# A four-layer graph kernel on Trainium2: gcn_first transposes its own rows, VectorE joins them, ScalarE scales the residual's part

## The reference, cut to what matters

```
def gcn_layer(x, edge_index, W, b, num_nodes):      # its own self loops are added once more
    deg  = segment_sum(1, dst);  dinv = rsqrt(deg);  norm = dinv[src] * dinv[dst]
    h    = x @ W
    return segment_sum(h[src] * norm, dst) + b
h   = relu(gcn_layer(x, edge_index, W1, b1))        # 128 -> 256
out = gcn_layer(h, edge_index, W2, b2)              # 256 -> 128
x   = layernorm(x + out)
```

## Time and profile before

| what | value |
|---|---|
| median of the runs | 5544.67 us |
| profiled execution | 5548.76 us |
| its span | 5547.0 us |
| mean granted TensorE clock | 0.932 |
| TensorE matmul busy | 4744.4 us (86%) |
| VectorE busy | 3861.5 us (70%) |
| GpSimd busy | 3017.4 us (54%) |
| ScalarE busy | 2782.1 us (50%) |

### The profile page before, as it was taken

One profiled execution on the slowest core, in us unless ns is written; L12 is line 12 of the kernel. 1 busy time (PEld: TensorE's weight loads), 2 busy tenths in 40 slices (PEclk: granted clock), 3 DMA queues, 4 the chain that ended last, 5 costly groups with the idle time before them and its releaser, 6 DMA issues. The chain is left out here.

```text
span 5547.0 us, 105377 instructions
## 1 busy us (share of the span) xinstructions
PE 4744.4 (86%) x27509; PEld 3749.1 (68%) x27509; DVE 3861.5 (70%) x11930; ACT 2782.1 (50%) x6703; POOL 3017.4 (54%) x2962
## 2 busy tenths in 40 slices
PE   4499996666799989999999997898799999447887
PEld 4488885555688867777777775777566666227887
DVE  8577775776688855555555554788688888885766
ACT  3644444656333322222222222788677777793545
POOL 0077765777677743333334333777466664007776
PEclk9999998777899989999999998999899999558999
DMA  4889994554577754444444443788877775784554
GB/s 149 274 246 275 273 270 142 151 147 147 177 237 238 236 170 151 153 154 150 150 147 153 152 153 92 223 250 249 245 221 222 222 225 181 261 294 132 153 148 141
DMA packets 551178, 1075.23 MB, mean 194 GB/s; under 512 B 110995, under 2 KB 118202, under 8 KB 547962
## 3 DMA queue, kind: packets, MB, share of 16 engines
q1 hardware_dynamic: 451194, 854.46, 46.5%
q0 software_dynamic: 99840, 219.14, 16.0%
HBM read 712.24 MB, written 360.98 MB: 193 GB/s over the span
## 5 line engine op out<-in xcount | busy, mean ns | idle before, releaser
L841 POOL DMA_INDIRECT s_rows<-t_h,s_index x416 | 525.4, 1263 | 831.5 <-DVE s_index L834 730.5
L841 POOL DMA_INDIRECT cb_rows<-t_x,cb_index x416 | 395.7, 951 | 451.4 <-DVE cb_index L834 327.7
L841 POOL DMA_INDIRECT g_rows<-t_x,g_index x416 | 425.9, 1024 | 384.9 <-issue 366.5
L841 POOL DMA_INDIRECT at_rows<-t_m,at_index x416 | 435.6, 1047 | 299.1 <-DVE at_index L834 189.8
L841 POOL DMA_INDIRECT s_rows<-t_v,s_index x416 | 405.1, 974 | 211.4 <-issue 120.4
L841 POOL DMA_INDIRECT s_rows<-t_x,s_index x416 | 420.5, 1011 | 154.8 <-issue 117.9
L841 POOL DMA_INDIRECT g_rows<-t_h,g_index x416 | 403.1, 969 | 171.1 <-issue 124.7
L905 PE MATMUL bank<-s_onehot,s_hi 128*128 128x80 f32 (+9 forms) x1758 | 436.7, 288 | 48.8 <-DVE s_lo L876 26.6
L1724 DVE TENSOR_TENSOR s_rout<-bank,s_x 128x512 f32<-128x512 f32 x98 | 67.9, 693 | 587.1 <-PE bank L1668 587.1
L905 PE MATMUL bank<-g_onehot,g_rows 128*128 128x80 f32 (+9 forms) x1172 | 299.6, 420 | 199.5 <-DMA g_rows<-t_h,g_index 193.5
L905 PE MATMUL bank<-s_onehot,s_lo 128*128 128x80 f32 (+9 forms) x1758 | 431.0, 285 | 0.0
(11 more groups left out here) (334 smaller groups left out, 13011.1 us busy)
## 6 DMA issues: line engine op xcount, KB each, us to landing
s_scale<-inv_d SPq DMA_DIRECT2D x196, 256.0 KB
t_h<-s_hout SPq DMA_DIRECT2D x98, 512.0 KB
s_own<-t_h SPq DMA_DIRECT2D x98, 512.0 KB
t_m<-s_mout SPq DMA_DIRECT2D x98, 264.0 KB
at_own<-t_m SPq DMA_DIRECT2D x98, 264.0 KB
t_x<-so_x SPq DMA_DIRECT2D x98, 256.0 KB, 4.7
g_own<-t_x SPq DMA_DIRECT2D x98, 256.0 KB
g_scale<-dinv_d SPq DMA_DIRECT2D x98, 256.0 KB
```

Of the source, the lines that this page charges most:

```text
L841: pool.indirect_dma_start(out=self.rows[:, self.ring(q) + k, :], out_offset=None, in_=self.table[0:NPAD, :], in_offset=bass.IndirectOffset ...
```

## The change

`gcn_first` no longer adds its own rows by products. TensorE transposes them into `bank[5]` (`flip`), ScalarE copies them to one of four SBUF tiles `own_t` (`turn`), and `scale_sums` becomes two instructions on VectorE: own_t times own1 plus the bank, then times the scale row. Because bank 5 is now taken, `down` uses bank 4 for every group. ScalarE's `scale` writes both `hout` and `rout` (with the new factor `dinv3_n` = own1 * dinv * dinv), eight instructions, and waits for the stores of both tiles; `rest` on VectorE becomes two plain additions. The lists of TensorE and ScalarE are reordered; VectorE's and SyncE's keep their lags.

```
-                dve.tensor_scalar(dinv2_n[:, :], dinv_n[:, :], own1[:, 0:1], None, ALU.mult)
+                dve.scalar_tensor_tensor(out=dinv3_n[:, :], in0=dinv_n[:, :], scalar=own1[:, 0:1],
+                                         in1=dinv_n[:, :], op0=ALU.mult, op1=ALU.mult)
...
+            own_t = ph.pair("own_t", [P, GRP], n=4)
...
-                    (0, lambda q: load(sp, q, own_rows[q.u][:, :], own_group(t_x0, q.t), loaded[q.u], e.summed)),
+                    (0, lambda q: load(sp, q, own_rows[q.u][:, :], own_group(t_x0, q.t), loaded[q.u], owned)),
...
+                def flip(q):
+                    pe.wait_ge(loaded[q.u], q.n * 16 + 16)
+                    if not (isinstance(q.t, int) and q.t < 1):
+                        pe.wait_ge(turned, q.t)
+                    for b in range(BLK):
+                        last = pe.transpose(bank[5][:, b * P:(b + 1) * P], own_rows[q.u][:, b * D:(b + 1) * D],
+                                            ident[:, :])
+                    last.then_inc(owned, 1)
+
                 def sums(q):
                     e.fetched(pe, q)
-                    pe.wait_ge(loaded[q.u], q.n * 16 + 16)
                     if not is_first(q.t):
                         pe.wait_ge(agged, q.t - 1)
-                    e.sum_by_feature(pe, q, [bank[q.u]], close=False)
-                    for b in range(BLK):
-                        last = pe.matmul(nodes(bank[q.u])[:, b, :], own_rows[q.u][:, b * D:(b + 1) * D],
-                                         id_own1[:, :], start=False, stop=(b == BLK - 1),
-                                         skip_group_check=True)
-                    last.then_inc(e.summed, 1)
+                    e.sum_by_feature(pe, q, [bank[q.u]]).then_inc(e.summed, 1)
...
                 def down(q):
                     pe.wait_ge(relued, q.t + 1)
-                    if not is_first(q.t):
-                        pe.wait_ge(scaled, q.t - 1)
+                    if not (isinstance(q.t, int) and q.t < 1):
+                        pe.wait_ge(scaled, q.t)
                     for b in range(BLK):
                         for h in range(2):
-                            last = pe.matmul(bank[4 + q.u][:, b * D:(b + 1) * D],
+                            last = pe.matmul(bank[4][:, b * D:(b + 1) * D],
...
-                over_groups(pe, [(1, sums), (5, down), (3, up)])
+                over_groups(pe, [(1, sums), (3, up), (5, down), (0, flip)])
...
+                def turn(q):
+                    act.wait_ge(owned, q.t + 1)
+                    if not is_first(q.t, 4):
+                        act.wait_ge(agged, q.t - 3)
+                    act.activation(own_t[q.r][:, :], bank[5][:, :], ACT.Copy).then_inc(turned, 1)
...
                     act.wait_ge(lowered, q.t + 1)
                     if not is_first(q.t):
                         act.wait_ge(st_h[q.u], q.n * 16)
-                        act.wait_ge(rested, q.t - 1)
-                    for b in range(BLK):
-                        last = act.activation(hout[q.u][:, b * D:(b + 1) * D],
-                                              bank[4 + q.u][:, b * D:(b + 1) * D], ACT.Copy,
-                                              scale=col(dinv_n, q.t * BLK + b))
+                        act.wait_ge(st_r[q.u], q.n * 16)
+                    for to, by in ((hout, dinv_n), (rout, dinv3_n)):
+                        for b in range(BLK):
+                            last = act.activation(to[q.u][:, b * D:(b + 1) * D], bank[4][:, b * D:(b + 1) * D],
+                                                  ACT.Copy, scale=col(by, q.t * BLK + b))
                     last.then_inc(scaled, 1)

-                over_groups(act, [(4, relu), (6, scale), (0, lambda q: e.take_hi(act, q))])
+                over_groups(act, [(6, scale), (1, turn), (4, relu), (0, lambda q: e.take_hi(act, q))])
...
                 def scale_sums(q):
+                    dve.wait_ge(turned, q.t + 1)
                     dve.wait_ge(e.summed, q.t + 1)
+                    if not is_first(q.t):
+                        dve.wait_ge(hidden, q.t - 1)
+                    dve.scalar_tensor_tensor(out=planes(agg[q.u]), in0=planes(own_t[q.r]), scalar=own1[:, 0:1],
+                                             in1=nodes(bank[q.u]), op0=ALU.mult, op1=ALU.add).then_inc(link, 1)
+                    dve.wait_ge(link, q.t + 1)
                     dve.wait_ge(loaded_s[q.u], q.n * 16 + 16)
-                    if not is_first(q.t):
-                        dve.wait_ge(hidden, q.t - 1)
-                    dve.tensor_tensor(planes(agg[q.u]), nodes(bank[q.u]), planes(scale_row[q.u]), ALU.mult)\
+                    dve.tensor_tensor(agg[q.u][:, :], agg[q.u][:, :], scale_row[q.u][:, :], ALU.mult)\
                        .then_inc(agged, 1)

                 def rest(q):
                     dve.wait_ge(scaled, q.t + 1)
                     dve.wait_ge(loaded_x[q.u], q.n * 16 + 16)
-                    if not is_first(q.t):
-                        dve.wait_ge(st_r[q.u], q.n * 16)
-                    for b in range(BLK):
-                        f = slice(b * D, (b + 1) * D)
-                        last = dve.scalar_tensor_tensor(out=rout[q.u][:, f], in0=hout[q.u][:, f],
-                                                        scalar=col(dinv2_n, q.t * BLK + b),
-                                                        in1=xin[q.u][:, f], op0=ALU.mult, op1=ALU.add)
-                    last.then_inc(link, 1)
-                    dve.wait_ge(link, q.t + 1)
+                    dve.tensor_tensor(rout[q.u][:, :], rout[q.u][:, :], xin[q.u][:, :], ALU.add).then_inc(link2, 1)
+                    dve.wait_ge(link2, q.t + 1)
                     dve.tensor_tensor(rout[q.u][:, :], rout[q.u][:, :],
                                       b2_r[:, :, :].rearrange("p b f -> p (b f)"), ALU.add)\
                        .then_inc(rested, 1)
```

More of the change, by code:

```diff
@@ L222, in build_program @@
     dinv_n = sb("dinv_n", [P, T * BLK])
-    dinv2_n = sb("dinv2_n", [P, T * BLK])
+    dinv3_n = sb("dinv3_n", [P, T * BLK])
     inv_n = sb("inv_n", [P, T * BLK])
@@ L1304, in gcn_first @@
             agged, relued, scaled, rested = ph.sem("agged"), ph.sem("relued"), ph.sem("scaled"), ph.sem("rested")
-            hidden, lowered, link = ph.sem("hidden"), ph.sem("lowered"), ph.sem("link")
+            hidden, lowered, link, link2 = ph.sem("hidden"), ph.sem("lowered"), ph.sem("link"), ph.sem("link2")
+            owned, turned = ph.sem("owned"), ph.sem("turned")
             st_h, st_r = ph.sems("stored_h"), ph.sems("stored_r")
@@ L1387, in scale_sums @@
                 def scale_sums(q):
+                    dve.wait_ge(turned, q.t + 1)
                     dve.wait_ge(e.summed, q.t + 1)
-                    dve.wait_ge(loaded_s[q.u], q.n * 16 + 16)
                     if not is_first(q.t):
                         dve.wait_ge(hidden, q.t - 1)
-                    dve.tensor_tensor(planes(agg[q.u]), nodes(bank[q.u]), planes(scale_row[q.u]), ALU.mult)\
+                    dve.scalar_tensor_tensor(out=planes(agg[q.u]), in0=planes(own_t[q.r]), scalar=own1[:, 0:1],
+                                             in1=nodes(bank[q.u]), op0=ALU.mult, op1=ALU.add).then_inc(link, 1)
+                    dve.wait_ge(link, q.t + 1)
+                    dve.wait_ge(loaded_s[q.u], q.n * 16 + 16)
+                    dve.tensor_tensor(agg[q.u][:, :], agg[q.u][:, :], scale_row[q.u][:, :], ALU.mult)\
                        .then_inc(agged, 1)
```

## The result

The changed kernel took 6125.73 us (median of five runs, 6124.42 to 6133.81), the kernel before 5546.14 beside it (five runs). The ratio is 1.1053, with a 95% interval of 1.104 to 1.1065: slower by 10.5%, 580 us. The forecast was 6050, with a range of 5920 to 6180. On a second chip of the same speed the changed kernel took 6124.43 us, ratio 1.1049 (1.103 to 1.1067). The profiled execution took 6133.81 us, its span is 6132.0.

A forecast was written before the change was run, and what follows sets the result against it. TensorE and GpSimd were both taken as full before; the loop's 91 x 11.2 = 1019 us, plus 31 and 10, end the stage at 1368 instead of 862, +505 us: median 5544.7 becomes 6050, range 5920 to 6180.

The forecast's parts named there:

- period: In gcn_first, one turn of the loop from scale to scale: 11.2 us, against 5.5 to 5.8 before.
- landing: In gcn_first's loop, from issue of the rout store until it has landed and releases the next scale: 3.4 us.
- five last periods: In gcn_first, scale(93) to scale(97), without take_hi, lo or turn: 5 x 6.1 = 31 us.
- last scale to the next stage: At gcn_first's end: 8.9 us before the change, 10 with four more instructions.
- The bound and the mechanism: In gcn_first, scale(q+1) waits for the store of rout(q-1), a loop within one period, engines mostly waiting: +505 us.
- The bounds of the landing: For gcn_first's rout store: 2.0 us below, 4.7 us above, giving 5915 to 6175 us for the program.
- rival a: In gcn_first, the loop holds and TensorE joins it at a lower clock: some 100 us more, 6150 to 6200; chance 0.10.
- The 38 us that TensorE was to save: In gcn_first, four transposes replace eight products' weight loads: 0.39 us less for each of 98 groups, gone in the loop.
- at least nothing, at most 26 us: VectorE's cost in gcn_first: net +0.27 us a group, 26 us over 98 groups if it were the bound.
- Rival (b): In gcn_first, the store has landed when scale comes and GpSimd is the bound: +10 us, 5555; chance 0.05.
- 30 us for longer gathers: In gcn_first, four VectorE instructions with two SBUF inputs instead of two lengthen gathers: 416 x 0.073 = +30 us.
- Rival (c): In gcn_first, faster: TensorE's 38 us come back whole, 5507 us; chance 0.03.

The follow-up runs named there:

- e1b: Changed kernel with four buffers of rout in place of two, on chip A: 5540.17 us, ratio 0.9997 to the kernel before.
- e5: Changed kernel with SyncE issuing the store of rout ahead of the load of x and store of hout, chip A: 5823.5 us, ratio 1.0506.
- e4b: Changed kernel with own rows added by products again, no transposes or join, residual still on ScalarE, chip C: 6917.78 us, ratio 1.0432.
- e4: Changed kernel with own rows added by products again, no transposes or join, residual still on ScalarE, chip B: 6829.31 us, ratio 1.044.
- e1: Changed kernel with four buffers of rout in place of two, on chip B: 6578.98 us, ratio 1.0079 to the kernel before.

## Why the prediction was right, step by step

| step | forecast | one period | mean over 91 |
|---|---|---|---|
| ScalarE: scale, turn, relu, high part | 4.42 | 4.43 (803.29 to 807.72) | 4.36 |
| VectorE: low part, two additions | 2.08 | 2.19 (807.72 to 809.91) | 2.08 |
| SyncE: to the issue of the rout store | 1.29 | 1.29 (809.91 to 811.20) | 1.25 |
| landing, to the next scale | 3.4 | 4.64 (811.20 to 815.84) | 4.47 |
| period | 11.2 | 12.55 | 12.16 (305.79 to 1412.37) |
| five last periods | 31 | | 26.5 (to 1438.8) |
| last scale to the next stage | 10 | | 8.0 |

**The bound and the mechanism** held: GpSimd and TensorE no longer set the time, but a loop does that no engine's busy time shows, and e1b, which opens just that loop, gives back all of the slowdown. **The mis-sized term is the landing.** The step "I take 3.4, near the row with the same three transfers in the same order" used the stage's end, where the trace has a load of x 0.9 us behind the store and the next store 2.4 us behind, and where no gather has run since 817.8 us. In the steady period the loads of the own rows and of the scale row follow 0.7 and 1.3 us behind, gathers run, and it is 4.5 (4.3 from the issue until the store has landed). That accounts for the miss: 1.07 us more from the landing and 0.11 less from the other terms are 0.96 in the period, so 91 x 0.96 = 87 us more, 4 and 2 less from the tail, 2 less since scale(1) came at 305.79: the stage ends at 1447 in place of 1368, and the program takes 76 us more than forecast.

**The bounds of the landing** held, in part by luck. The row of 4.7 us was taken for loads of x, but `t_x<-so_x` has the table on the left: it is the store of a tile of 256 KB to `t_x0`, issued right behind a load. Read so, it is a row of a store in steady state with another transfer just ahead, and by it the period would be 12.5 us. The lower bound of 2.0 us is from the stores of `sage_first`; the trace of the kernel before gives no landing for the stores of `gcn_first` itself.

**What sets the landing.** e5, e4b and the changed kernel form a series for this one store, in medians: 2.2 us with nothing just ahead, 3.7 behind x and hout, 4.5 behind both and with two loads close behind. What stands ahead is worth more than a microsecond: e5 changed only that order. For the last 0.8 us the traces show two conditions, read and not tested. One is the distance of the next load, by the stores of e4 and e4b above. The other is the gathers: at the end of the changed kernel's own stage, after the last gather (1367.16), a store with both loads 0.65 and 1.05 us behind is seen after 3.4 us, and so are its neighbours (3.4 to 3.6).

```profile
1387.36 0.43 SPq L970 DMA_DIRECT2D r<-g_rout  x1
1388.01 0.36 SPq L966 DMA_DIRECT2D g_own<-t_x  x1
...
1390.77 1.14 ACT L1392 ACTIVATE g_hout<-bank,dinv_n 128x128 f32<-128x128 f32 x4 [6.20 <-DMA r<-g_rout]
```

So the 3.4 us of the forecast is what such a store takes with no gather beside it, and the row of the stage's end was such a case. In e5 a load 0.6 and a store 1.1 us behind did not lengthen 2.2, with gathers running.

The Trainium skill, DMA: Bandwidth & Descriptors, section "Anatomy of one DMA — SWDGE (gpsimd) path", gives a formula for DMAs that GpSimd issues, by which a lone 256 KB store takes 2.6 us, an estimate. SyncE issues this one; the trace comes near the estimate where the store stands first (2.2 to the next scale, 2.0 to the landing), and has 4.3 to the landing in the changed kernel.

**TensorE (rival a)** did not join the loop. The clock did fall, 1.00 to 0.78 in the same stretch, in which TensorE is now idle for 37 of 98 us, and `down` takes 3.78 us in the period shown, in place of 1.95 before (at 500.60). But scale waited for `down` only 11 us in the whole stage, 7 of them in its last periods. The 38 us that TensorE was to save do not show here: four loads took 0.87 us, with the clock down. In e1b, at full clock, the saving shows as idle time.

**VectorE** costs nothing that can be told in e1b, as forecast (at least nothing, at most 26 us).

**Rival (b)'s condition** was made in e1b, and its end is right in kind: no change, GpSimd bound. Its 30 us for longer gathers were wrong: the mean went from 1024 to 1028 ns, 2 us in all. It counted the instructions with two inputs in SBUF as two before and four after, and left out the four on line 1402, which have two as well: by time they are 0.83 + 1.17 + 0.69 = 2.69 us a group before, and 0.82 + 0.68 + 0.69 + 0.69 = 2.88 after. That this explains the 4 ns is argued, not tested.

**Rival (c)** fell: with the loop open, 98 x 0.39 us of TensorE's time gave 0.9997.

## What to carry to other kernels

Before an instruction with a wait is moved to another engine, write down what stands behind it in that engine's list, and follow it until you come back to the wait or do not: three loops stood in these kernels (12.2, 6.1 and 6.5 us a period), and no busy share shows one. Where a loop passes through a store, more buffers of that tile open it, and until then the store's place in its queue is part of the period. Take a landing from a row with the same traffic: the same neighbours ahead and behind, and gathers running if they run in the loop. In a row `out<-in`, look which side is the table before you call it a load.

## What the runs showed of the hardware that was not expected

- The same 256 KB store took 2.2, 3.7 or 4.5 us to be seen, in the medians of e5, e4b and the changed kernel, by what was issued around it; in the changed kernel itself 4.5 while gathers run and 3.4 to 3.6 in the four periods after the last one.
- A gather that begins inside a VectorE instruction with two inputs in SBUF can take 1.39 us, the next 0.94 (810.80 and 812.49, above). In the changed kernel 38 of the 88 that begin so in this stage take over 1.2 us, and none of the other 328 does. The Trainium skill, SBUF — State Buffer, section "Who interferes with whom", says that such an instruction contends with GpSimd's reads of SBUF, and infers that it does not stall descriptor generation. By these rows the issue of an indirect DMA is stretched. Its indices lie in SBUF and have to be read, so this may be the read and need not be the generation; which of the two isn't shown.
- Chips differ: the kernel before takes 5542, 6536 or 6636 us, and e1's kernel, which costs 0.0% on the first, costs 0.8% on the second.
